# The last mixture-of-experts stage: every token through every expert, or tokens gathered into 39 blocks of 128 rows per expert

## The reference, cut to what matters

```python
x = x + _L3_xattn_ref(_layernorm(x), ctx_2048, ...)
x = x + _L3_ffn_ref(_layernorm(x), gate_w, expert_gate, expert_up, expert_down, shared_gate, shared_up, shared_down)

logits = x @ gate_w.T                                  # 256 -> 8
probs = softmax(logits)
routing_weights, selected = top_k(probs, 2)
routing_weights = routing_weights / (routing_weights.sum() + 1e-20)
combine = sum over the two of one_hot(selected) * routing_weights
out = silu(x @ shared_gate.T) * (x @ shared_up.T) @ shared_down.T
g = einsum('nh,eih->nei', x, expert_gate)              # all 8 experts, I = 176
u = einsum('nh,eih->nei', x, expert_up)
y = einsum('nei,ehi->neh', silu(g) * u, expert_down)
out = out + einsum('neh,ne->nh', y, combine)
```

## Time and profile before

| what | value |
|---|---|
| median of 3 runs | 2653.41 us (2653.03 to 2657.87) |
| the profiled execution, its span | 2653.4 us |
| PE busy | 2388.2 us, 90% of the span |
| DVE busy | 1787.8 us, 67% |
| ACT busy | 1545.0 us, 58% |
| POOL busy | 618.1 us, 23% |
| mean granted TensorE clock | 0.965 of full |
| last stage | from 2293.2 us (its first load is issued) to the end, 360 us |

### The profile page before, as it was taken

One profiled execution on the slowest core, in us unless ns is written; L12 is line 12 of the kernel. 1 busy time (PEld: TensorE's weight loads), 2 busy tenths in 40 slices (PEclk: granted clock), 3 DMA queues, 4 the chain that ended last, 5 costly groups with the idle time before them and its releaser, 6 DMA issues. The chain is left out here.

```text
span 2653.4 us, 49484 instructions
## 1 busy us (share of the span) xinstructions
PE 2388.2 (90%) x18480; PEld 1595.6 (60%) x18480; DVE 1787.8 (67%) x4455; ACT 1545.0 (58%) x2791; POOL 618.1 (23%) x674
## 2 busy tenths in 40 slices
PE   6977999999999978779879877999999999899998
PEld 5654666666566644457746665555555555566666
DVE  6856777675434438867567598999999999632321
ACT  4644666665333326634434357999999999522222
POOL 2214334433121213332132214111111111121111
PEclk9989999999999989989989998999999999899999
DMA  4120000000200021021010143766767666300000
GB/s 148 46 88 7 13 9 9 19 5 5 88 24 24 9 91 52 17 77 43 18 46 29 46 130 125 118 115 115 119 116 129 112 118 115 81 16 13 20 5 12
DMA packets 318716, 157.24 MB, mean 59 GB/s; under 512 B 265216, under 2 KB 314384, under 8 KB 317456
## 3 DMA queue, kind: packets, MB, share of 16 engines
q1 hardware_dynamic: 318480, 154.09, 25.1%
HBM read 66.48 MB, written 23.07 MB: 34 GB/s over the span
## 5 line engine op out<-in xcount | busy, mean ns | idle before, releaser
L2755 DVE CUSTOM_DVE_ANT_0 arena<-psum,attend_zero,queries_step 128x1024 f32<-128x1024 f32 x512 | 623.0, 1280 | 13.8 <-PE psum L2804 12.8
L2729 ACT ACTIVATE attend_ex<-arena,attend_mx 128x2048 uint16<-128x2048 f32 x256 | 521.8, 2038 | 6.3 <-issue 3.3
L1515 PE MATMUL psum<-arena,moe_tokT 128*128 128x512 f32 (+2 forms) x896 | 361.9, 549 | 2.9 <-DVE moe_h L1402 2.8
L2804 PE MATMUL psum<-keys_turned,queries_ahead 96*128 96x512 bf16 x1024 | 320.0, 395 | 41.0 <-DVE attend_mx L2755 25.4
L2829 PEld LDWEIGHTS psum<-values,attend_pw 128*128 128x128 f16 x4096 | 178.7, 97 | 125.4 <-issue 10.7
L1515 PEld LDWEIGHTS psum<-arena,moe_tokT 128*128 128x128 f32 x896 | 166.7, 192 | 139.3 <-issue 121.1
L1402 DVE TENSOR_TENSOR moe_h<-moe_sg,psum 128x512 f32<-128x512 f32 (+1 forms) x112 | 69.9, 624 | 264.3 <-PE psum L1515 259.4
L1249 ACT ACTIVATE moe_sg<-psum 128x512 f32<-128x512 f32 (+1 forms) x112 | 61.3, 548 | 292.7 <-PE psum L1515 288.4
L2707 POOL TENSOR_SCALAR attend_mx<-attend_mx 128x1 f32<-128x1 f32 x256 | 73.4, 287 | 573.9 <-DVE attend_mx L2755 573.9
L2820 PE MATMUL psum<-keys_turned,ident_b 96*128 96x512 bf16 x510 | 195.6, 384 | 0.0
L1537 PE MATMUL psum<-arena,moe_hT 128*128 128x256 f32 (+1 forms) x800 | 178.9, 380 | 2.7 <-ACT moe_hT L1261 1.6
(11 more groups left out here) (454 smaller groups left out, 4675.5 us busy)
## 6 DMA issues: line engine op xcount, KB each, us to landing
residual<-stored_rows SPq DMA_DIRECT2D x48, 128.0 KB, 1.7
queries_turned<-queries_rows SPq DMA_DIRECT2D x16, 384.0 KB, 3.2
queries_ahead<-queries_turned SPq DMA_DIRECT2D x16, 384.0 KB, 4.4
arena<-in_moe SPq DMA_DIRECT2D x1, 5704.0 KB, 18.1
arena<-in_gqa SPq DMA_DIRECT2D x1, 5440.0 KB, 16.5
arena<-in_moe SPq DMA_DIRECT2D x1, 4360.0 KB, 13.6
xatt_ct<-in_ctx_T SPq DMA_DIRECT2D x32, 128.0 KB, 2.3
residual<-stored_rows SPq DMA_DIRECT2D x16, 256.0 KB, 2.1
```

What stands on the lines that cost most here:

```text
L1515: last = nc.tensor.matmul(bank[:, q % 2, 0:size], tokT[:, i % 2, j, ic], wt[:, ic, at:at + size], start=ic == 0, stop=ic == DC - 1)
L2729: nc.scalar.activation(ex[:, u % ER:u % ER + 2], kept[:, u % KR:u % KR + 2], ACT.Exp, bias=mx[:, t % 2, h, 2:3], scale=-1.0, accum_out=sum ...
L2755: nc.vector.tensor_tensor_reduce(kept[:, u % KR], S[:, u % 2], zero[:].to_broadcast([P, UK]), steps[:, t, h:h + 1], 3.0e38, ALU.add, ALU.m ...
L2804: last = nc.tensor.matmul(S[:, u % 2, b * 512:(b + 1) * 512], qt[:, t % 2, h * P:(h + 1) * P], KT[:, c:c + 4, h // 2], start=True, stop=True)
```

## The change

The last `moe` call is replaced by a new function, `mixture3`, that computes the same output sparsely.

- In front, pair by pair as before: projection, norm, logits, and here also one tile of the shared expert for each pair (`front_shared = NI`, so tiles 0 to 7). The routing is done for groups of tiles (`GROUPS`): `choose` finds the two experts of each token, `rank` counts with small matmuls how many tokens ahead chose the same expert, and `place` makes from it the row that the token gets in a table in memory, `spread`. POOL scatters each tile's 128 rows twice, once for each chosen expert, by an indirect transfer (32 in all).
- Then the shared tiles 8 to 15 (`blocks_at = B`), all ahead of the blocks. `blocks` works out for each of `NB = 39` blocks which expert's weights it takes and at which row it lies (`bi`). 39 is the most that 4096 rows in 8 ranges of whole blocks can need, and all 39 are always computed.
- The blocks: SP reads a block's row from `bi` into a register and loads 128 rows; PE reads the expert's place into a register, turns the rows, multiplies gate and up (352 columns together), turns the hidden layer, multiplies down; DVE copies the result, and SP stores it over the same rows.
- At the end POOL gathers for each tile the two results of each token (32 indirect transfers), DVE weights and adds them (`combine`), and SP stores.
- `spread` is filled with zeros ahead of use: `clear_rows`, 17 transfers of 1024 rows (1 MB), one in each iteration of the loop of `gqa`.
- The weights of the stage are laid out anew, as 12,688 words for each partition where there were 11,408.

```diff
+ROWS_SPREAD = (E * B + E) * P
...
+def clear_rows(sp, k, i):
+
+
+    n = ROWS_SPREAD // (B + 1)
+    rows = k["spread"][i * n:(i + 1) * n].rearrange("(r p) d -> p r d", p=P)
+    sp.dma_start(rows, k["zeros"][:].unsqueeze(1).to_broadcast([P, n // P, D])).then_inc(k["rows_cleared"], 16)
 
...
+                    clear_rows(sp, k, i)
...
+def mixture3(nc, k, x_in, src_in, out, spread, arena, hand):
...
+    NB = B * P * 2 // P + E - 1
+    XI = 2 * I
+    CH = I // 2
+    WORDS = DC * XI + 2 * D
+    STRIDE = B * P
+    GROUPS = [(0, 4), (4, 8), (8, 12), (12, 14), (14, 16)]
+    SHARED_CHUNKS = [(0, P), (P, P), (2 * P, ISH - 2 * P)]
+    RR_, YR = 4, 4
+    front_shared = NI
+    blocks_at = B
+    with ExitStack() as ctx:
...
+            def load_rows(n):
+                if n >= RR_:
+                    sp.wait_ge(s["rows_turned"], n - RR_ + 1)
+                at = sp.value_load(bi[0:1, 1, n:n + 1], min_val=0, max_val=ROWS_SPREAD - P)
+                sp.dma_start(rows[:, n % RR_], spread[bass.ds(at, P)]).then_inc(s[f"rows_loaded{n % RR_}"], 16)
+                return at
+
+            def keep(n, at):
+                sp.wait_ge(s["block_kept"], n + 1)
+                sp.dma_start(spread[bass.ds(at, P)], yk[:, n % YR]).then_inc(s[f"kept_stored{n % YR}"], 16)
+
+            def store(t):
+                sp.wait_ge(s["y"], t + 1)
+                sp.dma_start(out[t], y[:, t % 4]).then_inc(s[f"stored{t % 4}"], 16)
+
+            load_h(1)
...
+            for n in range(NB + 3):
+                if n < NB:
+                    place[n] = load_rows(n)
+                if n >= 3:
+                    keep(n - 3, place[n - 3])
+            for t in range(B):
+                store(t)
...
+            def scatter(g):
+                if g == 0:
+                    pool.wait_ge(k["rows_cleared"], (B + 1) * 16)
+                pool.wait_ge(s["placed"], g + 1)
+                for t in range(*GROUPS[g]):
+                    pool.wait_ge(s["tok"], t // PAIR + 1)
+                    for c in range(2):
+                        nc.gpsimd.indirect_dma_start(out=spread[:, :], out_offset=bass.IndirectOffsetOnAxis(ap=at_i[:, c, t:t + 1], axis=0),
+                                                     in_=tok[:, t], in_offset=None).then_inc(s["scattered"], 16)
+
+            def gather(t):
+                if t >= 4:
+                    pool.wait_ge(s["y"], t - 3)
+                for c in range(2):
+                    nc.gpsimd.indirect_dma_start(out=yg[:, t % 4, c], out_offset=None, in_=spread[:, :],
+                                                 in_offset=bass.IndirectOffsetOnAxis(ap=at_i[:, c, t:t + 1], axis=0)).then_inc(s[f"gathered{t % 4}"], 16)
...
+            nc.gpsimd.iota(index[:], pattern=[[-1, E]], base=E, channel_multiplier=0, allow_small_or_imprecise_dtypes=True)
+            nc.gpsimd.iota(cum[:, 0], pattern=[[B, E]], base=0, channel_multiplier=0, allow_small_or_imprecise_dtypes=True)
+            nc.gpsimd.iota(upto[:], pattern=[[1, E], [-1, E]], base=1, channel_multiplier=0, allow_small_or_imprecise_dtypes=True)
+            nc.gpsimd.iota(count[:], pattern=[[1, NB]], base=0, channel_multiplier=0, allow_small_or_imprecise_dtypes=True).then_inc(s["tables"], 1)
+            for i in range(NI):
+                rstd(i)
+                if i == 0:
+                    clear_spent(nc, k)
+                if i + 1 < NI:
+                    bias(i + 1)
+                for g in group_after(i - 3):
+                    scatter(g)
+            for i in range(NI - 3, NI):
+                for g in group_after(i):
+                    scatter(g)
+            for r in range(4):
+                pool.wait_ge(s[f"kept_stored{r}"], (NB - r + YR - 1) // YR * 16)
+            for t in range(B):
+                gather(t)
+
...
+            def choose(g):
+                a, b = GROUPS[g]
+                m = b - a
+                spots = index[:].unsqueeze(1).to_broadcast([P, m, E])
+                prob, tied, rest = rt[:, 2, a:b], rt[:, 3, a:b], rt[:, 4, a:b]
+                dve.wait_ge(s["exped"], g + 1)
+                chained(nc.vector.tensor_reduce(rs[:, 1, a:b], rt[:, 1, a:b], X, ALU.add))
+                chained(nc.vector.reciprocal(rs[:, 2, a:b], rs[:, 1, a:b]))
+                chained(nc.vector.tensor_tensor(prob, rt[:, 1, a:b], wide(rs[:, 2, a:b], m), ALU.mult))
+                for c in range(2):
+                    left = prob if c == 0 else rest
+                    chained(nc.vector.tensor_reduce(rs[:, 3 + c, a:b], left, X, ALU.max))
+                    chained(nc.vector.tensor_tensor(tied, left, wide(rs[:, 3 + c, a:b], m), ALU.is_equal))
+                    chained(nc.vector.tensor_tensor(tied, tied, spots, ALU.mult))
+                    chained(nc.vector.tensor_reduce(rs[:, 5, a:b], tied, X, ALU.max))
+                    chained(nc.vector.tensor_tensor(pick[:, c, a:b], tied, wide(rs[:, 5, a:b], m), ALU.is_equal))
+                    if c == 0:
+                        chained(nc.vector.scalar_tensor_tensor(rest, pick[:, 0, a:b], -2.0, prob, ALU.mult, ALU.add))
+                chained(nc.vector.tensor_tensor(sel[:, a:b], pick[:, 0, a:b], pick[:, 1, a:b], ALU.add))
+                for t in range(a, b):
+                    chained(nc.vector.tensor_tensor(cum[:, t + 1], cum[:, t], sel[:, t], ALU.add))
+                nc.vector.memset(k["scratch"][:, 2:3], 0.0).then_inc(s["chosen"], 1)
+                chained(nc.vector.scalar_tensor_tensor(rs[:, 6, a:b], rs[:, 3, a:b], 1e-20, rs[:, 4, a:b], ALU.add, ALU.add))
+                chained(nc.vector.reciprocal(rs[:, 7, a:b], rs[:, 6, a:b]))
+                chained(nc.vector.tensor_tensor(wt[:, :, a:b], rs[:, 3:5, a:b], rs[:, 7, a:b].unsqueeze(1).to_broadcast([P, 2, m]), ALU.mult))
+
...
+            def blocks():
+                total, near, blocks_e, lead, ends = (be[:, m] for m in range(5))
+                eb = [P, NB, E]
+                dve.wait_ge(s["rank_psum"], len(GROUPS))
+                chained(nc.vector.tensor_scalar(near, TOTAL, 1.0 / P, 0.49609375, ALU.mult, ALU.add))
+                chained(nc.vector.tensor_scalar(near, near, MAGIC, -MAGIC, ALU.add, ALU.add))
+                chained(nc.vector.tensor_tensor(blocks_e, near, cum[:, 0], ALU.subtract))
+                chained(nc.vector.tensor_scalar(lead, blocks_e, -1.0, float(B), ALU.mult, ALU.add))
+                chained(nc.vector.scalar_tensor_tensor(bm[:], upto[:], 0.5, blocks_e.unsqueeze(1).to_broadcast([P, E, E]), ALU.is_gt, ALU.mult))
+                chained(nc.vector.tensor_reduce(ends, bm[:], X, ALU.add))
+                chained(nc.vector.tensor_tensor(bc[:], ends.unsqueeze(1).to_broadcast(eb), count[:].unsqueeze(2).to_broadcast(eb), ALU.is_le))
+                chained(nc.vector.tensor_reduce(bs[:, 0], bc[:], X, ALU.add))
+                chained(nc.vector.tensor_tensor(bc[:], bc[:], lead.unsqueeze(1).to_broadcast(eb), ALU.mult))
+                chained(nc.vector.tensor_reduce(bs[:, 1], bc[:], X, ALU.add))
+                chained(nc.vector.tensor_scalar(bs[:, 2], bs[:, 0], float(E - 1), float(WORDS), ALU.min, ALU.mult))
+                chained(nc.vector.tensor_tensor(bs[:, 3], bs[:, 1], count[:], ALU.add))
+                chained(nc.vector.tensor_scalar(bs[:, 3], bs[:, 3], float(P), None, ALU.mult))
+                nc.vector.tensor_copy(bi[:], bs[:, 2:4]).then_inc(s["block_table"], 1)
...
+            def block_keep(n):
+                dve.wait_ge(s["block_y"], n + 1)
+                if n >= YR:
+                    dve.wait_ge(s[f"kept_stored{n % YR}"], n // YR * 16)
+                nc.vector.tensor_copy(yk[:, n % YR], YB).then_inc(s["block_kept"], 1)
...
+            def combine(ts):
+                for t in ts:
+                    dve.wait_ge(s[f"gathered{t % 4}"], (t // 4 + 1) * 32)
+                    dve.wait_ge(s["residual"], t + 1)
+                    if t >= 2:
+                        dve.wait_ge(s["y"], t - 1)
+                    nc.vector.scalar_tensor_tensor(acc[:, t % 2], yg[:, t % 4, 0], wt[:, 0, t:t + 1], xk[:, t], ALU.mult, ALU.add).then_inc(s["first_added"], 1)
+                for t in ts:
+                    dve.wait_ge(s["first_added"], t + 1)
+                    if t >= 4:
+                        dve.wait_ge(s[f"stored{t % 4}"], t // 4 * 16)
+                    nc.vector.scalar_tensor_tensor(y[:, t % 4], yg[:, t % 4, 1], wt[:, 1, t:t + 1], acc[:, t % 2], ALU.mult, ALU.add).then_inc(s["y"], 1)
+
+            dve.wait_ge(s["tables"], 1)
+            for i in range(NI + 1):
+                if i < NI:
+                    if i < front_shared and i >= 1:
...
+            for t in range(front_shared, blocks_at):
+                shared_product(t)
+                if t > front_shared:
+                    residual(t - 1)
+            residual(blocks_at - 1)
+            for n in range(NB + 3):
+                if 1 <= n <= NB:
+                    block_product(n - 1)
+                if n >= 3:
+                    block_keep(n - 3)
...
```

(57 more changed lines are left out.)

412 lines of the change are left out of this document (403 added, 9 removed).

## The result

| | before | after |
|---|---|---|
| median of 4 runs each | 2654.62 us (2653.03 to 2657.87) | 2816.43 us (2812.78 to 2818.50) |
| span of the profiled execution | 2653.4 us | 2815.8 us |

The change makes the kernel 6.1% slower: ratio 1.061, 95% interval 1.0595 to 1.0625. The forecast was 2800. It gave slower a chance of 0.93 and a range of 2710 to 2885.

A forecast was written before the change was run, and what follows sets the result against it. PE's arithmetic was taken to bound the old kernel, waits on row loads the new blocks. 2443 to the blocks, 285 + 22 + 2 for them, 42 + 3.4 gathers, 3.7 end: 2801, stated 2800 us; range 2710 to 2885.

The forecast's parts named there:

- The order on SP's queue: Blocks: load n+1 queues behind store n-3, which waits for PE's iteration n, so load latency idles PE 35 times.
- The forecast's cycle: Blocks: one turn with an exposed load takes 8.15 us, 35 times, 285 us.
- The seven blocks without an exposed load: Blocks: seven iterations that wait for no load, about 3.2 us each, 22 us.
- The part off PE: Block cycle: DVE copy, SP wake, store issue, register path and row load, 4.25 us together.
- The register path: Block cycle on SP: register load taken as 1.0 us, between 0.1 and 1.7, plus 0.15 for three register instructions.
- PE's part: Block cycle: PE's work per block, 2.7 us at full clock, 5.1 at the lower level, middle 3.9 taken.
- Rival B: Blocks: PE at its lower clock throughout, each cycle 1.2 us longer, total 2843 us; chance 0.13.
- down 1.30: Front: the shared expert's three down matmuls on PE, 1.30 us per tile, following two ACT copies.
- Scatters, clearing, tables at nothing: POOL's scatters and new tables priced 0; clearing in gqa priced 0, at most 5 us.
- Rival C: POOL's indirect transfers cost 3.1 us each, lengthening gathers and delaying the front, total 2887 us; chance 0.10.
- E: Blocks: loads run ahead of PE thanks to four row buffers, total 2616 us, faster by 37; chance 0.05.
- D: Unseen costs all low: register load 0.1, full clock, cycle 6.05, gathers 24 us, total 2710 us; chance 0.12.

The follow-up runs named there:

- e1: Changed kernel with SP storing block n-5 instead of n-3 behind the load of block n; 2594.57 us.
- e6: Changed kernel with constant row numbers on SP for block loads and stores, in place of numbers read from a table; 2789.80 us.
- e2: Changed kernel with ten bf16 matmuls that nobody reads added on PE behind each block's down; 2734.17 us.
- e3: Changed kernel with DVE's residual add of the front moved ahead of the next pair's stats and norm; 2805.32 us.
- e10: Changed kernel with the edits of e1 and e3 alone, all shared tiles still ahead of the blocks; 2594.49 us.
- e4: Changed kernel with shared tiles 8 to 15 moved behind the blocks, beside the gathers; 2786.96 us in three executions.
- e7: Changed kernel with the edits of e1, e3 and e4 together; 2587.72 us.
- e5: Changed kernel with SP storing block n-4 instead of n-3 behind the load of block n; 2627.37 us.
- e8: e7 with ACT's copies of the hidden values moved ahead of exp in the front; 2591.36 us.
- e9: Changed kernel with the edits of e1 and e3, four shared tiles ahead of the blocks and four beside the gathers; 2583.45 us.

## Why the prediction was right, step by step

| | predicted | measured | difference |
|---|---|---|---|
| blocks begin (`turn_rows` 0) | 2443 | 2452.8 | +9.8 |
| blocks to their last store landed | 309 | 315.1 | +6.1 |
| gathers and last sums | 45.4 | 44.4 | -1.0 |
| end | 3.7 | 3.5 | -0.2 |
| sum | 2801 | 2815.8 | +14.7 |

**The order on SP's queue: right, and shown.** The forecast rested on the store of block n-3 standing between PE's end and the load of n+1. The waits name it (128.3 us in 35 waits, all before `turn_rows`), and e1, which changes nothing but that order, takes them all away. The forecast's cycle was 8.15, measured 8.53: 35 times 0.38 is 13 us. The seven blocks without an exposed load and the landing took about 7 us less than their 22 + 2.

**The sizes inside the cycle: two errors that mostly cancel.** The part off PE was priced at 4.25 us and is 3.67. Copy 0.42, wake and store issue came out within 0.1 of what was worked out from the earlier trace rows, the transfer at 2.0 against 2.2. The register path was the term without a row, priced 1.15 over a plain issue, and e6 measures 0.76. PE's part was put at 3.9, the middle between 2.7 and 5.1. It is 4.86. Over 35 turns that is 34 us too little on PE and 20 too much off it. That the sum came out near is luck; the mechanism is not. Both ends were good: e2 shows 2.74 at full clock, and the turn at 0.50 took 5.17. Wrong was the choice of the middle. The earlier trace rows had shown the drop after one idle stretch of 4.79 us, and the mean of 0.84 in the earlier trace rows, over a stretch that was busy 45% of its time, was from another loop and did not carry over. Here a gap of 3.6 us comes in every turn, and the mean is 0.60 with PE busy 58% (172 of 297 us). Rival B's clock was nearly what happened; its 2843 was not reached mainly because the off-PE part was cheaper.

The Trainium skill (TensorE: Matmul & The Clock Gate, HAM oscillation) describes a loop in which each slice of matmuls begins at the lower clock after waiting for a transfer. This case's trace agrees: `turn_rows` takes 0.69 us behind each of the 35 waits, where it took 0.38 with no wait ahead, and the clock is 0.60 over the blocks. It is 1.00 with the same chain of transfers once e2's fillers stand in the gaps.

**The start of the blocks: 9.8 us under-priced.** The stage began 1.9 us earlier than priced (first token turned at 2303.1, not 2305.0). The front took 107.4 us, to 2410.5, against the 98 of the forecast; an iteration, from project to project, took 9.3 to 16.1 us, where 9.5 was the price of a plain one and 14 of one that ends a group. The eight shared tiles took 42.3 against 40. So the error lies in the front. The front's step "down 1.30" was taken as ready once ACT had copied. In the trace of the changed kernel it waits for another:

```profile
2336.48 1.66 DVE L1903 TENSOR_SCALAR moe_tok<-moe_xk,moe_mv,moe_sm 128x256 f32<-128x256 f32 x2 [0.74 <-POOL moe_sm L1757]
2338.06 0.41 DVE L1981 TENSOR_TENSOR moe_xk<-psum,moe_xk 128x256 f32<-128x256 f32 x1
...
2338.62 2.26 PE L2137 MATMUL psum<-arena,moe_hsT 128*128 128x256 f32 x6 [3.79 <-DVE moe_xk L1981]
```

`shared_down(t)` needs the bank that `residual(t-1)` reads, and that add stands on DVE behind the norm of the next pair. 24.6 us in 6 waits. The prediction followed the data but not the freeing of the bank. And the front's lower clock (0.79) had no term at all. How the 9.4 us that the front took too long divide between the two is not shown: in e3 and e10 that wait is gone, and in e10 nothing was gained by it.

**Scatters, clearing, tables at nothing: right.** Scatters take 0.96 us each and no one in the front waits for them; in `gqa` PE's busy time is within 1.6 us of before. It holds while other work lies behind them: without it the last scatters kept PE waiting 10.75 us in e4 and 12.5 in e7.

**Gathers: right.** One each 1.30 us in the mean (2767.9 to 2808.2 for 32), against the 1.3 taken between 0.43 and 3.1. That the middle of so wide a span was met is luck too. Rival C is out. With the first one issued 2.65 us after PE's last product is copied, the tail is 48 us in which PE has nothing to do.

**Rivals.** E, the faster side, was excluded by the order on SP, as argued; e1 then makes E true by that one edit, and its 2616 was 21 us too high, nearly all of it in the blocks (2440.3 to the first gather at 2543.5, 103 us, against 124). D fails on the clock, on the register path (0.76 against 0.1 and 0.15 for the register instructions) and on the gathers (40.3 us against 24).

## What to carry to other kernels

In a queue served in order, ask of every store what it waits for and which load is queued behind it. Row buffers buy nothing if the load of the next block stands behind a store that waits for the newest result; two iterations more between them were worth 222 us here. Where each iteration of PE is short and ends in a wait as long as the one here (3.6 us in 8.5), price its matmuls at the lower clock; the shorter waits of e5 left it up. And doubt a sum of savings that were each measured alone: all four such sums here came out too good, by 10 to 45 us.

## What was not expected of the hardware

- A register load from SBUF on SP took 0.27 us (262 to 478 ns over 39), its register operations 0.15. The store and the load behind it were issued 1.12 us apart with it and 0.36 without, so the engine pays 0.76. The Trainium skill (DMA: Bandwidth & Descriptors, Latency and other measured facts) gives a floor of about 600 ns for such a load; the row of the load alone is under half of it, the whole path is above.
- An indirect transfer of 128 rows of 1 KB holds POOL for 0.95 us, and the next is issued 1.26 us after it in most cases. All 32 gathers came at 1.30 us in the mean, with DMA at 0.40 of its engines.
- Gaps of 3.6 us in each turn of 8.5 brought the granted clock to 0.60; gaps of 0.9 to 1.8 us in about every second turn left it at 0.98.
- Idle stretches of ACT of 4.4 to 9.8 us beside POOL's gathers, with what the code waits for done long before their end, came twice in each of e7, e8 and e9 and not in e4. They are unexplained.
